# Second attention of a four-stage kernel: both kinds of heads stacked, attended and copied together, and the order of a step rewritten

## The reference

```
v = x @ w_v + b_v
wq, wk = split(x @ w_wqk + b_wqk)      # windowed: 4 windows of 64 tokens
wdots = einsum(wq, wk) * SCALE + w_bias
wout = softmax(wdots) @ v              # inside a window
q, k = split(x @ w_qk + b_qk)          # global: all 256 tokens
dots = einsum(q, k) + g_bias
out = softmax(dots) @ v
return (wout + out) @ w_out + b_out
```

## Time and profile before

| | |
|---|---|
| median of 3 runs | 1747.52 us (1744.76 to 1750.48) |
| the profiled execution | 1759.47 us, span 1757.7 us, clock 0.954 |
| PE busy over the span | 1489.7 us (85%) |
| DVE busy | 1189.0 us (68%) |
| ACT busy | 1000.8 us (57%) |
| POOL busy | 785.2 us (45%) |

### The profile page before, as it was taken

The page is one execution under the profiler, slowest core; times in us unless marked ns, Lnnn a source line. Parts: engine busy times, 40 slices in busy tenths (PEclk is TensorE's granted clock), DMA queues, the critical chain, the costliest instruction groups (busy, mean ns, idle before and its releaser), DMA issues. The chain is left out here.

```text
span 1757.7 us, 37146 instructions
## 1 busy us (share of the span) xinstructions
PE 1489.7 (85%) x12057; PEld 1147.2 (65%) x12057; DVE 1189.0 (68%) x3253; ACT 1000.8 (57%) x1682; POOL 785.2 (45%) x1008
## 2 busy tenths in 40 slices
PE   2599999999999587999169998999899999689997
PEld 1467767767766466899046666666666666478886
DVE  2367777767766555999556777777777766556676
ACT  1377777777776254777126565665656666333332
POOL 8765464685662343998562334343333220100111
PEclk9899999999999788999569999999999999789999
DMA  5000000010010110222211111111111111000000
GB/s 192 21 20 19 16 19 17 25 32 19 25 35 19 33 58 12 73 68 64 77 42 35 35 35 40 31 35 33 33 33 33 31 30 30 1 1 7 12 12 18
DMA packets 75074, 60.29 MB, mean 34 GB/s; under 512 B 17088, under 2 KB 71104, under 8 KB 74560
## 3 DMA queue, kind: packets, MB, share of 16 engines
q1 hardware_dynamic: 70848, 50.21, 10.0%
q0 software_dynamic: 4096, 8.40, 1.7%
HBM read 20.01 MB, written 13.37 MB: 19 GB/s over the span
## 5 line engine op out<-in xcount | busy, mean ns | idle before, releaser
L1274 DVE TENSOR_REDUCE a_qt<-a_ps_d 128x2 fp32r<-128x512 f32 (+1 forms) x384 | 263.6, 689 | 140.8 <-PE a_ps_d L1059 96.3
L537 ACT ACTIVATE a_p<-a_ps_s 128x1024 f32<-128x1024 f32 x256 | 263.1, 1029 | 63.8 <-PE a_ps_s L395 59.4
L638 DVE TENSOR_REDUCE a_qt<-a_ps_d 128x2 fp32r<-128x512 f32 x256 | 171.6, 685 | 105.8 <-PE a_ps_d L406 105.5
L799 POOL TENSOR_TENSOR a_rn<-a_ss,a_half 128x16 f32<-128x16 f32 x64 | 185.9, 2913 | 1.4
L1186 ACT ACTIVATE a_pg<-a_ps_s 128x1024 f32<-128x1024 f32 x128 | 131.8, 1031 | 12.5 <-PE a_ps_s L1033 7.4
L1059 PE MATMUL a_ps_d<-a_kpad,a_qs 128*128 128x512 f32 x256 | 126.2, 493 | 13.6 <-DVE a_qt L1274 12.5
L406 PE MATMUL a_ps_d<-a_kpad,a_qs 128*128 128x512 f32 x256 | 119.7, 471 | 15.5 <-DVE a_qt L638 13.9
L413 PE MATMUL a_ps_o<-a_p,a_v 128*32 128x256 f32 x2048 | 125.3, 384 | 1.0 <-ACT a_p L537 1.0
L1024 PE MATMUL a_ps_a<-ident,a_qt 128*128 128x128 f32 x512 | 107.1, 291 | 10.8 <-ACT a_qsm L1180 8.0
L1505 POOL COPY a_v<-a_vt 128x64 f32<-128x64 f32 x64 | 15.4, 240 | 212.8 <-PE a_ps_o L1136 212.8
L1180 ACT CAST a_ks<-a_ps_a 128x256 fp32r<-128x256 f32 x128 | 47.6, 372 | 110.0 <-PE a_ps_a L1024 101.7
(11 more groups left out here) (359 smaller groups left out, 4280.1 us busy)
## 6 DMA issues: line engine op xcount, KB each, us to landing
a_kpad<-a_ks SPq DMA_DIRECT2D x512, 32.0 KB, 1.8
a_kpad<-a_kq SPq DMA_DIRECT2D x256, 32.0 KB, 1.9
f_xin<-xs SPq DMA_DIRECT2D x39, 128.0 KB, 2.1
ys<-f_yout SPq DMA_DIRECT2D x39, 128.0 KB, 2.1
w<-in_w SPq DMA_DIRECT2D x2, 2304.0 KB, 11.3
out_x<-X SPq DMA_DIRECT2D x8, 256.0 KB, 2.3
xs<-f_zero SPq DMA_DIRECT2D x15, 128.0 KB
wgu<-in_wgu SPq DMA_DIRECT2D x1, 1152.0 KB
```

Source lines behind the costliest of these rows:

```text
L537: nc.scalar.activation(probs[:, u % 2, 2 * c:2 * c + 2, :, :].rearrange("p a b c -> p (a b c)"), ps_s[:, n % 2, :], ACT.Exp).then_inc(exp_ ...
L638: nc.vector.tensor_reduce(qt2[:, k % 2, 2 * part:2 * part + 2, SHIFT], bank(k, f"m{part}")[:, :].rearrange("p (a b) -> p a b", b=S), AX.X, ...
L799: nc.gpsimd.tensor_tensor(rn[:, part * c:(part + 1) * c], ss[:, part * c:(part + 1) * c], half[:, 0:c], ALU.pow).then_inc(rn_ready, 1)
L1274: nc.vector.tensor_reduce(dst, src, AX.X, ALU.max, negate=True).then_inc(d_done, 1)
```

## The change

The second attention is changed on all engines; no other stage is.

- M, K and Q are stacked for both kinds at once: four transposes and one copy of 512 columns each, so that `ps_a` changes hands three times a step, not six (plus xT or yT).
- The attend of both kinds is one block of 16 matmuls into one bank, copied by one copy (`ot`), transposed by four transposes (O) and read by DVE in one reciprocal and one multiply over both halves.
- A DMA moves the keys of both kinds: 4 issues a unit, not 8, with the same bytes.
- The step is in a new order on PE: M, m0, (wq, q or v), attend, global scores 0, m1, K, O, global scores 1, m2, (wk, k), m3, Q, m4, (yT or xT), m5, windowed scores, (op). M now waits for DVE to have read m5 of the step before, and the attend waits for the windowed exponential of the step before.
- ACT copies xT and yT behind the windowed exponential, at the end of its step. DVE does most of its work of a batch between m0 and m1, reads O between m1 and m2, and does the sum of the two kinds behind m2.

The core of the diff:

```diff
-    A_ORDER = ("Mg", "Kw", "Mw", "Qg", "yT", "xT", "Kg", "Qw")
-    D_ORDER = ("m0", "wq", "q", "v", "m1", "wk", "m2", "k", "m3", "Og", "m4", "Ow", "m5", "op")
+    A_ORDER = ("M", "K", "Q", "yT", "xT")
+    D_ORDER = ("m0", "wq", "q", "v", "m1", "O", "m2", "wk", "k", "m3", "m4", "m5", "op")
...
+                for kind in (WINDOWED, GLOBAL):
+                    for t in range(TPB):
+                        part = stacked(src[:, (u // NG) % 2, kind, t * H + t0:t * H + t0 + G, :])
+                        last = nc.tensor.transpose(ps_a[:, kind * S + t * P:kind * S + (t + 1) * P], part, ident[:, :])
+                last.then_inc(a_full, 1)
...
                 if unit(k - 1):
-                    pe.wait_ge(d_done, st.at(lambda k: d_count(k - 1, "m3")))
-                    stack(st, "Mg", qt, k - 1)
+                    pe.wait_ge(d_done, st.at(lambda k: d_count(k - 1, "m5")))
+                    stack(st, "M", qt, k - 1)
...
+                if unit(k - 2):
+                    pe.wait_ge(exp_done, st.at(lambda k: chunk(k - 1, 2)))
+                    pe.wait_ge(v_ready, st.at(lambda k: k - 1))
+                    attend(k - 2)
...
             for st in steps(act):
                 if unit(k - 1):
-                    copy_a(st, "Mg", qsm[:, GLOBAL, :])
+                    copy_a(st, "M", qsm[:, :, :].rearrange(flat))
+                if unit(k - 2):
+                    act.wait_ge(o_full, st.at(lambda k: k - 1))
+                    nc.scalar.copy(ot[:, :], ps_o[:, :]).then_inc(o_copied, 1)
...
                 if unit(k - 1):
-                    wait(act, w_full, st.at(lambda k: k - 2))
                     act.wait_ge(scores_full, st.at(lambda k: chunk(k, 2)))
                     nc.scalar.activation(pw[:, (k - 1) % 2, :, :, :].rearrange("p a b c -> p (a b c)"),
                                          ps_s[:, (chunk(k, 2) - 1) % 2, :], ACT.Exp).then_inc(exp_done, 1)
+                if r == 2 and batch(b - 1):
+                    copy_a(st, "yT", yT[:, :])
+                if r == 1 and batch(b + 2):
+                    copy_a(st, "xT", xT[:, :])
```

More of the change, by code:

```diff
@@ L1100, in _ @@
                         pe.wait_ge(consts, 1)
[L1101 to L1104, removed]
+                    pe.wait_ge(stacks_ready, st.at(lambda k: 2 * ((k + 2) // NG) + 2))
+                    stack(st, "K", kt, k + 2)
                 if unit(k - 2):
[L1106 to L1113, removed]
@@ L1114, in _ @@
-                maxima(st, 1)
-                if unit(k - 1):
[L1116 to L1120, removed]
+                    wait_d(st, "O")
+                    pe.wait_ge(o_copied, st.at(lambda k: k - 1))
+                    for n in range(2 * TPB):
+                        last = nc.tensor.transpose(bank(k, "O")[:, n * P:(n + 1) * P], ot[:, n * P:(n + 1) * P],
+                                                   ident[:, :])
@@ L1131, in _ @@
-                if unit(k - 2):
-                    pe.wait_ge(exp_done, st.at(lambda k: chunk(k - 1, 2)))
-                    pe.wait_ge(g_copied, st.at(lambda k: k - 1))
-                    for t in range(TPB):
-                        for j in range(G):
-                            last = nc.tensor.matmul(ps_o[SLOT * j:SLOT * (j + 1), t * P:(t + 1) * P],
-                                                    v32[:, (k - 2) % KEEP, t, j, :], pw[:, k % 2, j, t, :],
-                                                    start=True, stop=True)
-                    last.then_inc(w_full, 1)
+                maxima(st, 3)
@@ L1140, in _ @@
+                if unit(k + 1):
+                    stack(st, "Q", qt, k + 1)
+                maxima(st, 4)
                 if r == 2 and batch(b - 1):
@@ L1344, in _ @@
[L1344 to L1351 removed]
+                maxima(1)
@@ new lines, in _ @@
+                maxima(2)
+                if unit(k - 2):
+                    dve.wait_ge(d_done, st.at(lambda k: d_count(k, "O")))
+                    g = (k - 2) % NG
+                    dst = out[:, ((k - 2) // NG) % 2, :, g * G * HD:(g + 1) * G * HD]
+                    one, two = [both[:, n * TPB * G:(n + 1) * TPB * G, :].rearrange("p (t h) d -> p t (h d)", t=TPB)
+                                for n in range(2)]
+                    nc.vector.tensor_tensor(dst, one, two, ALU.add).then_inc(out_ready, 1)
```

241 lines of the change are left out of this document (102 added, 139 removed).

## The result

The changed kernel takes 1765.84 us (median of 4 runs, 1765.04 to 1767.46), the kernel before 1748.62 us beside it (4 runs, 1744.76 to 1750.48). The ratio is 1.0103, with a 95% interval of 1.0083 to 1.0122: slower by 17 us. The prediction had 1789.5 us, 42 slower, so the sign is right, the time lies in its range (1764 to 1812) by less than 2 us, and the size is less than half of what was forecast.

A forecast was written before the change was run, and what follows sets the result against it. PE was taken to bound the kernel. 41.09 against 38.20 us a batch gave +37.6 us over 13 batches, plus +4 to +5 for the 12 steps outside: 1747.5 + 42 = 1789.5 us, range 1764 to 1812.

The forecast's parts named there:

- the copies' place: ACT copies xT and yT after the windowed exponential, so M waits for `ps_a`: 2.66 us a batch, or 35 us.
- The walk: Start-by-start timing of the new second-attention step on PE, DVE and ACT: 8.95 + 10.77 + 11.15 + 10.22 = 41.09 us a batch.
- Rival 1: M finds `ps_a` free, so xT's and yT's copies cost nothing: 38.4 us a batch, about 1752 us, no change; 6%.
- the walk of PE and DVE from m1 to m5: After the attend's start, m2's reading at 4.41 us; m5 at 6.38, 6.60, 7.03 and 7.15 us for r = 0 to 3.
- DVE's lateness at m5: DVE's work ahead of m3's reading delays m5 on PE by 0.6 to 0.9 us a step.
- the base: The unchanged second attention takes 38.20 us a batch, the mean of 13 batches in the profiled execution of 1759.47 us.
- rival 3: PE's idle stretches lower its clock to 0.9: some 3.3 us more a batch, +43 us, 1833 us; 5%.
- Rival 2: Fewer hand-overs let PE run closer to its 32.7 us: 36.5 us a batch, -22 us, 1725 us; 7%.
- Rival 4: DVE's work of a batch outlasts the attend, between m0 and m1: 1805 us; 12%.
- the two copies' rows: Sign: PE's waits ahead of M name `a_xT` and `a_yT`, 1.1 to 1.9 us from the windowed scores' end, about 15 times each.
- the distances of 10.8 and 11.1 us: Sign: windowed exponentials (L1199) start 9.0, 10.8, 11.1 and 10.2 us apart, 41.1 us for the four.
- The waits ahead of L1061: Sign: PE waits for DVE's `a_qt` ahead of this line, some 0.5 to 0.9 us in each step.

The follow-up runs named there:

- the fillers: The changed kernel with 12 unread extra transposes on PE behind the windowed scores in the two steps whose M waits: 1758.90 us, 1.0057 of the kernel before.
- the kernel with two reads: The changed kernel with ACT's copies of yT and xT first and DVE's reciprocal and multiply of O done for each kind apart: 1740.14 us, ratio 0.9904.

## Why the prediction was right in sign and wrong in size

**Right: the copies' place.** "ACT is in order, so the copy of xT follows ... M needs `ps_a` and waits for that copy." The walk priced it at 1.14 + 1.52 = 2.66 us a batch; measured are 2 x 1.38 = 2.76, and one edit that moves the copies alone takes 47 us off, the clock's part included. Rival 1 (the copies don't bite) is refuted.

**Wrong: the walk of PE and DVE from m1 to m5.** This step failed. Its sum was 41.09 us a batch; the four distances are 38.16. The attends of one batch, with the first m5 behind the fourth, in the timeline of PE:

```profile
1181.59 1.07 PE L1086 MATMUL a_ps_o<-a_pg,a_v 128*32 128x256 f32 x16 [0.29 <-ACT a_pw L1199]
...
1202.21 1.07 PE L1086 MATMUL a_ps_o<-a_pg,a_v 128*32 128x256 f32 x16
1211.58 1.07 PE L1086 MATMUL a_ps_o<-a_pg,a_v 128*32 128x256 f32 x16
...
1215.17 0.87 PE L1056 MATMUL a_ps_d<-a_kpad,a_qs 128*128 128x512 f32 x2
...
1217.22 0.50 PE L1061 MATMUL a_ps_d<-a_kpad,a_qs 128*128 128x512 f32 x1 [0.36 <-DVE a_qt L1250]
...
1219.75 1.07 PE L1086 MATMUL a_ps_o<-a_pg,a_v 128*32 128x256 f32 x16 [0.29 <-ACT a_pw L1199]
```

With the attend at 1191.67 shown above, the steps take 10.08 (r = 1), 10.54 (r = 2), 9.37 (r = 3) and 8.17 us (r = 0), where the walk has 10.77, 11.15, 10.22 and 8.95: 0.6 to 0.85 too long in every step, with the copies' wait and without it. Most of that is already there at m5: in the last step it starts 1217.22 - 1211.58 = 5.64 us behind the attend, in the walk 6.38; over the four steps m5 takes 2.47 of the 2.93 us. The rest lies behind m5, mostly in distances of the same kind (from M to the attend 1191.67 - 1190.41 = 1.26 us, in the walk 1.32, of which 0.03 was a slip: by its own rows going into an attend costs 0.36 - 0.23 = 0.13, not 0.16). What is there at m5 has two parts, most of it a record's length, or a gap read in the first attention, taken for a distance between starts here. On PE, four transposes took 0.36 to 0.43 and not 0.46, and a maximum with transposes behind it 0.24 and not 0.34, so m2 starts at 3.59 (1215.17) and not 3.87. On DVE I put everything from m2 to m3 behind each other at the length of its record. The timeline of DVE in the changed kernel:

```profile
1214.03 0.69 DVE L1250 TENSOR_REDUCE a_qt<-a_ps_d 128x2 fp32r<-128x512 f32 x1 [0.38 <-PE a_ps_d L1056]
1214.90 0.26 DVE L1342 RECIPROCAL a_ro<-a_ps_d 128x16 f32<-128x16 f32 x1 [0.18 <-PE a_ps_d L1130]
1215.19 0.29 DVE L1344 TENSOR_TENSOR a_both<-a_ps_d,a_ro 128x128 f32<-128x128 f32 x1
1215.61 0.69 DVE L1250 TENSOR_REDUCE a_qt<-a_ps_d 128x2 fp32r<-128x512 f32 x1
1216.22 0.22 DVE L1354 TENSOR_TENSOR a_out<-a_both 128x64 f32<-128x64 f32 x1
1216.51 1.95 DVE L1250 TENSOR_REDUCE a_qt<-a_ps_d 128x2 fp32r<-128x512 f32 x3
```

m2's reading starts 4.03 us behind the attend and not 4.41: the 0.28 of PE, and 0.44 us from m2's matmul and not 0.54. The sum of the kinds (L1354) starts 0.61 us behind the start of m2's reading, not 0.69, and m3's reading 0.29 behind that, where the walk has 0.215 for the sum and 0.33 for the two aggregates between them. Three maxima together are 1.95 us: the first two cost about 0.63 each, and only the last its full 0.69. These DVE distances are 0.4 us of the 0.74 at m5. For PE the prediction had corrected for this lag (0.92 for a record of 1.09); for DVE it had not.

**Wrong in the same way: DVE's lateness at m5**, 0.6 to 0.9 us in each step of the walk. It is 0.4 us in about half of the steps (10.5 us in 27 waits), and taking DVE's work away gave 13.4 us over 64 steps where the clock had no part, 0.2 a step.

**Wrong: the base.** The 38.20 us of the first trace are those of an execution whose ACT was held up once a batch; the median of the runs has 37.60. The walk's difference was taken against the slow batch and added to the median of the others, which alone would have made the forecast 8 us too low.

**Underrated: the clock, rival 3 with its 5%.** It does fall after the wait for a copy, behind six of the 29 waits, but for some 3.4 us each time and at a cost of 9.6 us in the trace (6.8 in the timed medians), not 43. The sentence that 8% idle time and a clock of 1.00 speak against it judged by averages and overlooked that one idle of 1.38 us comes in one piece. The Trainium skill ("TensorE: Matmul & The Clock Gate", section "A second HAM failure mode: psum-queue depth-cycling") describes short idles between groups that make the clock oscillate; the windows from 1149.50 on and the fillers' 6.8 us agree with it.

**The account**, a batch: walked 41.09 - 38.20 = +2.89; less 2.93 for the walk, 2.47 of it up to m5; plus 0.60 for the base; plus 38.72 - 38.16 = 0.56 for the drops; that is +1.12, or +14.6 us over 13 batches. Around them +4 to +5 were expected and 17.2 - 14.6 = 2.6 came, with the sixth drop in it. Sum +17.2, as timed. The base and the drops, neither of them foreseen, took back 1.16 of the walk's 2.93 us a batch: that the time lies in the range, 1.8 us from its end, is luck.

**The rivals.** Rival 2 (grouping wins, 7%) was half right: its premise, "DVE's lateness is overestimated", held, but its 36.5 us a batch already count 2.7 for the copies' waits, and with these waits a batch without a drop takes 38.16. Nor did it lose to the copies: with them first it would have named 33.8, and 35.47 came. Of the 1.7 us between, 0.85 go with DVE's work behind the maxima (34.62) and 0.68 with the transposes behind m5 (33.94), so DVE's lateness and the wait for Q's copy were larger than its "share of the other waits". Rival 4 (DVE's work outlasts the attend) shows in none of the longest waits. Of the signs named ahead, the two copies' rows came as written, with 14 waits each; the distances of 10.8 and 11.1 us came as 10.5 and 10.3, and those of 9.0 and 10.2 both as 8.6. The waits ahead of L1061 came in about half of the steps and not in each, PEclk was 0.98 and not 1.00, and a batch stayed below the 39 us that I had named as the mark of being wrong.

## What to carry to other kernels

Where an engine works in order, a short instruction whose result frees a buffer for the busiest engine belongs ahead of a long one that still waits for its input, even if its own result is needed late: here 0.37 us of copy in the wrong place cost 47. A rearrangement is several changes, and one of them can hide the gain of the rest; look for the largest new wait and undo that alone before the whole is dropped. When a step is walked through, take distances between starts from a place where the same instructions stand back to back, on every engine, and compare with two executions of the base before a fraction of a microsecond a step is multiplied by 64.

## What the runs showed of the hardware

- In the changed kernel PE idles 1.38 to 1.47 us at 29 places. Behind six of them some 3.4 us at the lower level of the clock followed (0.50 from about 1151.4 on), mostly every third batch and at the same six places in both traces; behind the other 23 the clock stayed at 1.00. With twelve more transposes in the idle time it fell at none.
- DVE's reductions of 512 columns back to back start about 0.63 us apart, though each record is 0.69 (three together 1.95, at 1216.51 in the changed kernel).
- An instruction can start 1.2 to 1.6 us later than its data allows, at the same place of ten batches and in one execution of a kernel but not in another (ACT's copy of the attend, 588.2 against 580.1 us for the stretch). DVE's add of op in the kernel with two reads is late in the same way in ten batches of its one trace. All twenty start 0.9 to 1.5 us behind the end of POOL's gathers, and none is late in a batch without gathers. The cause was not found, as the same gathers ran without this in the other trace; the profile names as releaser "remote" or an instruction long done.
